# The last of eight passes of a two-stream decoder kernel written out behind the loop

## What is computed

```
x = x + L0_attn(layernorm(x))        # delta rule, chunks of 32, taps of 4, 7 and 25
x = x + L0_xattn(layernorm(x), ctx)  # 16 heads
x = x + L0_ffn(layernorm(x))
x = x + L1_attn(layernorm(x));  x = x + L1_xattn(..., ctx);  x = x + L1_ffn(...)   # last: 8 experts
x = x + L2_attn(...);  x = x + L2_xattn(..., ctx, mask);     x = x + L2_ffn(...)   # last: 14 experts
x = x + L3_attn(...);  x = x + L3_xattn(..., ctx, mask);     x = x + L3_ffn(...)   # scan; 8 experts, capacity 512
```

## The kernel before

| stream 0 in | stream 1's steps put there | w |
|---|---|---|
| L0_delta | L2_attn, L2_cross, L2_moe whole | 12 |
| L0_cross | L3_mamba 46 | 23 |
| L0_ffn, L1_attn | L3_mamba 35 | 19 |
| L1_mix, L1_moe | L3_cross, L3_moe whole | 14 |
| L2_attn, L2_cross, L2_moe | L0_delta whole, L0_cross 2 | 2 |
| L3_mamba | L0_cross 27, L0_ffn 7, L1_attn 19 | 43 |
| L3_cross, L3_moe | L1_attn 6, L1_mix, L1_moe whole | 26 |

## Time and profile before

### The profile page before, as it was taken

The page is one execution under the profiler, slowest core; times in us unless marked ns, Lnnn a source line. Parts: engine busy times, 40 slices in busy tenths (PEclk is TensorE's granted clock), DMA queues, the critical chain, the costliest instruction groups (busy, mean ns, idle before and its releaser), DMA issues. The chain is left out here.

```text
span 4993.3 us, 97444 instructions
## 1 busy us (share of the span) xinstructions
PE 4078.1 (82%) x38655; PEld 2833.0 (57%) x38655; DVE 3236.5 (65%) x8464; ACT 2059.6 (41%) x4978; POOL 671.0 (13%) x1030
## 2 busy tenths in 40 slices
PE   2688888888888898888888888888888888888883
PEld 1455565656556566656556565555656565555652
DVE  3467767576766757676775767677675767677661
ACT  1245353534435353444435353443535344353530
POOL 1010201102010111101020110102011010102002
PEclk9689889798888889888888988898898988798897
DMA  4000000000000000000000000000000000000013
GB/s 125 1 2 1 7 1 7 1 3 5 1 7 1 6 2 7 2 1 7 1 7 1 6 2 6 2 1 7 1 7 1 4 4 1 7 1 6 2 33 89
DMA packets 70922, 46.81 MB, mean 9 GB/s; under 512 B 13095, under 2 KB 67488, under 8 KB 70226
## 3 DMA queue, kind: packets, MB, share of 16 engines
q1 hardware_dynamic: 65024, 33.82, 2.4%
q0 software_dynamic: 2048, 3.85, 0.3%
q10 hardware_dynamic: 3378, 2.64, 0.2%
HBM read 30.14 MB, written 10.50 MB: 8 GB/s over the span
## 5 line engine op out<-in xcount | busy, mean ns | idle before, releaser
L728 PE MATMUL banks<-scratch 32*128 32x512 f32 x2112 | 584.3, 764 | 74.8 <-ACT scratch L1635 36.2
L838 ACT ACTIVATE scratch<-banks 128x512 f32<-128x512 f32 x528 | 276.5, 600 | 254.6 <-PE banks L762 254.4
L301 ACT ACT_TABLE_LOAD x293 | 375.9, 1283 | 10.1 <-PE banks L1055 4.9
L874 DVE TENSOR_REDUCE scratch<-banks 128x4 f32<-128x512 f32 x528 | 330.0, 683 | 59.5 <-PE banks L728 36.1
L728 PEld LDWEIGHTS banks<-scratch 32*128 32x128 f32 x2112 | 205.3, 214 | 255.6 <-issue 84.8
L1650 ACT ACTIVATE scratch<-scratch,ssm_A 128x256 f32<-128x256 f32 x512 | 229.5, 500 | 264.5 <-DVE scratch L1707 251.9
L1562 PE MATMUL banks<-scratch,w_ident 128*128 128x256 f32 x1024 | 282.6, 399 | 57.0 <-DVE scratch L1713 56.9
L1707 DVE TENSOR_TENSOR_SCAN scratch<-scratch 128x512 f32<-128x512 f32 x256 | 313.2, 1224 | 12.6 <-ACT scratch L1650 5.2
L1846 PE MATMUL banks<-scratch 32*32 32x32 f32 (+1 forms) x11152 | 251.8, 206 | 48.8 <-issue 28.1
L1846 PEld LDWEIGHTS banks<-scratch 32*32 32x32 f32 (+1 forms) x11152 | 219.6, 119 | 101.9 <-issue 73.0
L1192 PE MATMUL banks<-experts,scratch 128*128 128x128 f32 x1792 | 261.3, 294 | 9.1 <-ACT scratch L1228 6.3
(11 more groups left out here) (515 smaller groups left out, 8932.7 us busy)
## 6 DMA issues: line engine op xcount, KB each, us to landing
experts<-in_e_W SPq DMA_DIRECT2D x16, 256.0 KB, 5.4
w_e_W<-in_e_W SPq DMA_DIRECT2D x3, 704.0 KB
expert_in<-scratch SPq DMA_DIRECT2D x1, 2048.0 KB, 14.2
scratch<-expert_in SPq DMA_DIRECT2D x8, 256.0 KB, 4.6
expert_out<-scratch SPq DMA_DIRECT2D x8, 256.0 KB, 2.3
scratch<-residual SPq DMA_DIRECT2D x8, 256.0 KB
out<-scratch SPq DMA_DIRECT2D x8, 256.0 KB
experts<-in_e_w SPq DMA_DIRECT2D x1, 1792.0 KB, 7.8
```

The costliest lines, as they stand in the source:

```text
L301: act.preload_act_table_set(name)
L728: last = pe.matmul(row_tiles(t), lhs[r, col(s)], rhs[r, s], start=True, stop=letter == "S" and mask is None, skip_group_check=True)
L838: P.give(act.activation(pT[:, s % 2, j, :], t, ACT.Exp), f"{nm}.T{s}{j}")
L874: P.give(dve.tensor_reduce(negm[:, s, NI * j:NI * j + NI], row_tiles(t), X, ALU.max, negate=True), f"{nm}.S{s}{j}")
```

## The change

Four things. The loop runs seven passes, and an eighth is written out behind it as a stretch "last". In it stream 1 does only its first six sections of a pass, L2_attn to L3_moe, and neither stream loads another group; SP has no `landed` to wait for. The inputs lose the four appended sequences. And the eighth pass has strings of its own, LAST_TURNS, in which stream 1's six sections stand beside all twelve of stream 0. Read against the steps, PE's new string puts:

| stream 0 in | stream 1's steps put there | w |
|---|---|---|
| L0_delta | L2_attn, L2_cross whole | 16 |
| L0_cross | L2_moe 26 | 0 |
| L0_ffn, L1_attn, L1_mix | L2_moe 32 | 0 |
| L1_moe | L2_moe 4, L3_mamba 13 | 20 |
| L2_attn | L3_mamba 17 | 12 |
| L2_cross | L3_mamba 28 | 8 |
| L2_moe | L3_mamba 8 | 0 |
| L3_mamba | L3_mamba 15, L3_cross 17 | 77 |
| L3_cross, L3_moe | L3_cross 3, L3_moe 4 | 11 |

(two more w stand ahead of the first section, in both strings.) PE changes stream 166 times in the old string and 117 times in the new one.

```
--- before.py
+++ after.py
@@ -85,6 +85,27 @@
      "000011110000110010101110111111111111111111111111"),
     ("110001000010100010011010000000011001101100111111001111011001011111110000111100"),
     ("111000"),
+]
+LAST_TURNS = [
+    ("111ww0001000001111101111000110101100111111110000000000000000000000000000000011011001000011111111001111111111"
+     "1wwwwwwwwwwwwwwww1000001110111111100110011001110000000000000000001111011111001110000111011111001011000000000"
+     "00000000001100011111111000111111110000001110001wwwwwwww0000000001100000000000000000000000000001111000001wwww"
+     "w000000000wwwwwww0011111100100110000000000001100000000111110111wwwwwwwwwwww11110001111wwwwwwww00100001111111"
+     "000001111000111000000011111011110000000010000000000000000000000000000000000000000000000000000001111111000000"
+     "0111111110000001wwwwwww1110001wwww110000000000000011www0001100000w0000wwwwwwwwwww0000wwwww000000000000wwwwww"
+     "ww0000wwwwwwwwwwww0000wwwwwww0000w00000000wwwwww0wwwwwwwwwwww01111101111111100011wwwww01000000000000000wwwww"
+     "w011100010"),
+    ("111000000001111000011110111110000000000000000000000000000111110000001111110111100000001101111111001100101110"
+     "000000000111111001110000111111000001100000000001111111001110011100010000110000001111010011111111001000111000"
+     "001100000111000011010000011010000110010000000000000000000000000000000000000000000000100001000100000000000000"
+     "00110101000000000111100000000110010"),
+    ("110010111111000111111000111110000001100000000000001100000000000000000001110011000011111111111011000000110110"
+     "001001001010010000000000000001001010000000111000000000000000001001001000110100011100000000000000011100000000"
+     "000111100100000000000000011001100111001011111100111000000000001111100111111001110011010010000000000000000101"
+     "111100011111100100101101110000000000001111000100000000000000000000000000000000001011110000000111100100001100"
+     "000001010"),
+    ("110010000000001100100000000000011100000000111100001010"),
+    ("11001"),
 ]
 LENGTHS = 4
 EXP, SILU, GELU, LN = "exp_and_others", "silu_and_others", "gelu_and_others", "natural_log"
@@ -136,7 +157,7 @@
     w = {}
     cont = np.ascontiguousarray
     for n, m in (("x", "x"), ("ctx", "ctx_1024"), ("mask", "mask_BxSxS2_if1"), ("key_pad", "mask_BxS2_bk0")):
-        w[n] = np.concatenate([a[m], a[m][0:G * STREAMS]])
+        w[n] = a[m]
     for n in ("Wq", "Wk", "Wv", "Wb", "Wo"):
         w["d_" + n] = a["L0_attn_" + n]
     w["d_Wb_wide"] = cont(np.repeat(a["L0_attn_Wb"], DELTA_D, axis=1))
@@ -2279,7 +2300,8 @@
                     "L3_cross": lambda: cross3(f"{u}x3"),
                     "L3_moe": lambda: moe3(f"{u}e3"),
                 }
-                order = ROUND[u] if part == "round" else ROUND[u][ROUND[u].index("L0_delta"):] if FIRST[u] else []
+                start = ROUND[u].index("L0_delta") if FIRST[u] else len(SECTIONS)
+                order = {"first": ROUND[u][start:], "round": ROUND[u], "last": ROUND[u][:start]}[part]
                 sections = {name: makers[name]() for name in order}
                 at_v = TURN[u]
                 x_d, c_d, m_d = (a.rearrange("(g u s) t f -> u g t s f", u=STREAMS, s=G)[at_v]
@@ -2320,7 +2342,8 @@
                             yield
                         if name == "L3_moe" and engine == 4:
                             yield from stored(args[0], args[1])
-                            load(args[0], args[1] + 1)
+                            if part == "round":
+                                load(args[0], args[1] + 1)
                             yield
 
                 def landed(sp):
@@ -2373,7 +2396,7 @@
         def stretch(part, g):
 
             P = Psum(banks, filled, emptied)
-            turns = TURNS if part == "round" else [""] * 5
+            turns = {"first": [""] * 5, "round": TURNS, "last": LAST_TURNS}[part]
             tables.now = None
             groups = [make(P, part) for make in streams]
             with nc.Block() as block:
@@ -2399,15 +2422,17 @@
                         for load, _, _, _ in groups:
                             load(sp, 0)
                     in_turns(turns[4], P, groups, 4, sp, g)
-                    for _, landed, _, _ in groups:
-                        landed(sp)
+                    if part != "last":
+                        for _, landed, _, _ in groups:
+                            landed(sp)
 
             clear(turn_sems(groups))
             nc.all_engine_barrier()
 
         stretch("first", None)
-        with nc.Fori(0, NGROUPS) as g:
+        with nc.Fori(0, NGROUPS - 1) as g:
             stretch("round", g)
+        stretch("last", NGROUPS - 1)
 
         if "L3_moe" not in SECTIONS:
             return
```

## The result

The changed kernel takes 4861.36 us (median of 4 runs, 4855.53 to 4871.85) against 4992.42 us (4 runs, 4987.52 to 4996.94); the ratio is 0.974, with a 95% interval of 0.9718 to 0.9762. So 131 us are gone where 99 were forecast. The range of 4860 to 4926 just holds it, and the time lies where the rival "dense filling" put it (4853 to 4875), not at 4893.

What follows compares the result with a forecast made beforehand. The prediction took TensorE's ordered queue to bound the loop and a lone stream its own chain. A 465 us pass plus 1.5, against 562.3, saves 95.8, with the loop return 98.8: median 4893 us, range 4860 to 4926.

Steps and rivals of the forecast that it cites:

- dense filling: Last pass: the wider spread keeps TensorE at 85%, a pass of 425 to 447 us, 4853 to 4875; chance 0.15.
- What bounds the kernel: The loop is bound by TensorE's one ordered queue, one stream alone by its dependent chain; the changed pass lies between.
- what is removed: Six sections of stream 1 in the last pass, 105 to 130 us of TensorE work; eight loads costed at nothing.
- The seam: Entry to the last pass: one loop return becomes a fall through, 3.0 us less, between 0 and 4.
- The high bound: Last pass if spreading gains nothing: first half 285.5 us as before, second half alone 181 to 198, together 467 to 484.
- The chain alone: Stream 0's twelve sections in the last pass without the other stream's work: 378 to 395 us.
- the price by steps: Stream 0's second half alone, estimated at 0.41 us per foreign step taken away: 198 us.
- the one by ratio: Stream 0's second half alone, estimated by the first half's stretching of 1.45: 181 us.
- The section sum: Last pass timed along stream 0's sections, each between its time alone and its time before: 465 us.
- The slower clock: The thinner last pass falls to clock 0.75, a pass of 523 us, 4951; chance within 0.09 shared with a poor order.
- The blocking order: TensorE's queue waits at its 117 stream changes, over 1.5 us each: slower than before, 5002 us; chance 0.04.
- The unchanged chain: The last pass keeps stream 0's length, so only 13 us and the loop return are won: 4976; chance within 0.09.

Runs made afterwards that it cites:

- the run in the old order: The changed kernel with its eighth pass in the old packed order, the half pass still dropped: 4911.04 us, ratio 0.9829.
- the one with L2_attn and L2_cross only: The changed kernel without warming matmuls and without stream 1's L2_moe, L3_mamba and L3_cross in the eighth pass: a pass of 422.6 us.

## Why the prediction was right, and where it was off

**How right it was.** The median lies 1.4 us inside the range, and only because the range reached below the forecast's own 4875 into a rival's. The pass of 445.2 us is outside the 447 to 492 that were given 0.70. So the direction and the kind of gain were foreseen; that the number was held owes something to luck.

**What bounds the kernel; what is removed.** Right in kind. The removed work was 456.7 - 361.2 = 95.5 us of TensorE in place of 105 to 130. The 130 were the lead's, run at a clock of 0.75; why 105, a share by steps, was also too high isn't shown. That the eight loads cost nothing was not tested by itself.

**The seam.** Forecast 3.0 us, measured 2.85.

**The high bound.** Stream 0's second half alone: 181 to 198 forecast, 197.6 measured without the end's 1.5. The unspread pass: 467 to 484, measured 489.9 without the 1.5. The chain alone: 378 to 395, measured 393.6 with warming and 397.4 without. These were the sound part, and the price by steps was nearer than the one by ratio each time.

**The section sum**, 465 forecast, 443.7 measured (445.2 less the 1.5 of the end):

| | forecast | measured | off by |
|---|---|---|---|
| L0_delta, from the first root | 97 | 116.4 | +19.4 |
| L0_cross | 40 | 26.0 | -14.0 |
| L0_ffn, L1_attn, L1_mix | 58 | 42.4 | -15.6 |
| L1_moe | 37 | 33.3 | -3.7 |
| L2_attn, L2_cross | 71 | 71.9 | +0.9 |
| L2_moe | 46 | 34.9 | -11.1 |
| L3_mamba | 74 | 79.0 | +5.0 |
| L3_cross, L3_moe | 42 | 40.0 | -2.0 |

The step that failed is the price of stream 1's L2_moe, taken each time as matmul time paid on the path. It was added beside L0_cross to L1_moe (about 30 us over the lone sections) and cost nothing there. It was also taken off L0_delta whole (34.3 us), where in the packed order it had cost 133.1 - 115.2 = 18 us, by the run in the old order against the one with L2_attn and L2_cross only. (The loop's passes have 127 to 137 us for that L0_delta, so 18 is good to some 5.) The two errors partly cancel, which is why the sum looked reasonable. A third term, stream 0's own L2_moe at 46, was mis-sized too: beside eight scan steps it ran in 34.9, about what it takes alone (33.1).

**The median.** The forecast lay 32 us high: 21.2 of it in the pass, 1.9 in the loop's passes, 1.1 in the expert stage, and 7.7 because the profiled execution was this time 10.5 us above the median and not 2.8.

**The rivals.** Dense filling, given 0.15, is what happened: a pass of 445.2 within its 425 to 447, TensorE busy 84%. Its argument against itself, that VectorE is full beside the scan, isn't borne out as a cause: with VectorE busy 70.3 of 79.0 us in L3_mamba the scan cost 25 us in all, but the attention cost as much in L0_delta, where VectorE is busy 70.8 of 115.2. The slower clock fell: 0.87, and 0.86 without any warming, as the other stream's work keeps TensorE busy 84 and 81% of the pass. The Trainium skill, "TensorE: Matmul & The Clock Gate", Part 1, on idleness that throttles the array, does agree with L0_delta alone (0.53, TensorE busy 51%). The blocking order fell: the pass is 443.4 - 397.4 = 46 us over the chain, both without warming, at 117 changes of stream, 0.4 us each, far below the 1.5 that it needed. The unchanged chain fell with the run in the old order, whose pass is 71 us shorter than before's.

**The signs named in advance.** L2_attn began 218 us into the pass (forecast 232); the clock was over 0.8; TensorE was busy 84%, not 75 to 80; L2_attn and L2_cross stayed under 45 us; L3_mamba took 79 for "near 74"; and the first transfer came at 4718.35 in place of 4741.5.

## What to carry to other kernels

Where two streams share the engines, price the other's work by its kind and by what it lies beside, not by its TensorE time. Here L2_moe's 34 us of plain matmuls cost nothing beside cross-attention and attention and some 18 us when packed beside L0_delta, while the attention pair and the scan cost 25 us each, with 47 and 31 us of TensorE time. And see how far repeats of one stretch differ before a difference of a few us is read. When a half-filled stretch is left over, spreading the remaining work along the whole of the longest chain was worth 46 us beside the 71 of the work dropped. A return of the loop left VectorE idle about 3.2 us longer than straight code, and writing all passes out saved 7.4 us a pass, so in a loop of a few long passes writing all of them out is worth a try.

## What the hardware showed that was not expected

Adding matmuls made the chain's own matmuls faster: with L2_moe beside them the granted clock of four sections rose from 0.75 to 0.97, and they ended 5.2 us sooner (69.6 against 74.8 us) with 26 us of foreign matmuls taken in (144 of L2_moe's 168). Passes with the same instructions took 564 to 581 us; in the kernel before the shortest was granted 0.88 and the longest 0.85. And VectorE's idle time was 4.03 to 5.07 us at the returns of the loop in all twelve kernels that have one, against 1.06 to 1.31 at every entry from straight code. The Trainium skill, "Runtime: NRT & Kernel Launch", "Instruction fetch mechanics", says that a taken branch whose target isn't in the instruction window has to fetch it before execution can go on. The rows agree in kind; that it is the fetch is not shown by them.
